# Moving the start of the table lookup on TensorE in a two-layer graph network from slot 19 to slot 12

## What is computed

```
msgs = z[edge_dst] @ Wd + z[edge_src] @ Ws + edge_weight[:, None] * ww[None, :] + bm
agg = segment_max(msgs, edge_dst);  hidden = relu(z @ W1a + agg @ W1b + b1);  out = hidden @ W2 + b2
x = layernorm(x + out)
x = layernorm(x + sage(x))      # two mean aggregations over the same edges, with a relu between
```

## Time and profile before

| | us |
|---|---|
| median of three runs (1100.16 to 1101.87) | 1100.61 |
| the profiled execution | 1098.6 |
| its span, from the first to the last instruction | 1096.8 |
| TensorE busy in the span | 1020.9 |
| VectorE busy | 852.8 |
| POOL busy | 739.7 |
| ScalarE busy | 671.0 |

### The profile page before, as it was taken

One profiled execution on the slowest core, in us unless ns is written; L12 is line 12 of the kernel. 1 busy time (PEld: TensorE's weight loads), 2 busy tenths in 40 slices (PEclk: granted clock), 3 DMA queues, 4 the chain that ended last, 5 costly groups with the idle time before them and its releaser, 6 DMA issues.

```text
span 1096.8 us, 25699 instructions
## 1 busy us (share of the span) xinstructions
PE 1020.9 (93%) x7183; PEld 756.1 (69%) x7183; DVE 852.8 (78%) x2994; ACT 671.0 (61%) x1741; POOL 739.7 (67%) x782
## 2 busy tenths in 40 slices
PE   4898989999999999999999999998988989899997
PEld 4576667777777777776767777766666666657786
DVE  6598788888878878887979888987877877645465
ACT  3345778988887778877867887433233333313664
POOL 7767777777777777777777777777777777201332
PEclk9898999999999999999999999999999999999999
DMA  8654434344334434434444443543444353545321
GB/s 204 166 130 114 96 98 103 94 100 119 95 102 106 107 104 107 101 94 128 107 102 92 104 94 98 144 107 88 115 132 104 101 148 99 147 127 164 80 59 42
DMA packets 130203, 121.29 MB, mean 111 GB/s; under 512 B 24126, under 2 KB 115573, under 8 KB 130053
## 3 DMA queue, kind: packets, MB, share of 16 engines
q1 hardware_dynamic: 103624, 70.53, 24.5%
q0 software_dynamic: 23328, 47.82, 18.0%
q10 hardware_dynamic: 3101, 1.21, 0.5%
HBM read 105.60 MB, written 13.88 MB: 109 GB/s over the span
## 4 chain that ended last, share of the span: by engine, by line
PE 48%; POOL 27%; issue 13%; ACT 4%; DVE 3%; DMA 2%; ACTq 2%; DVEq 0%; SPq 0%
POOL area L1100 27%; PE bank L1833 9%; PE bank L1735 8%; PE bank L1959 7%; PE bank L1724 5%; PE bank L1802 4%; PE bank L1675 4%; PE bank L1714 3%; PE bank L1663 2%; PE bank L1924 2%; ACT area L949 1%; PE bank L1910 1%; DMA area<-zs_d,area 1%; ACT hot_r L957 1%; ACTq L889 1%
## 5 line engine op out<-in xcount | busy, mean ns | idle before, releaser
L1100 POOL DMA_INDIRECT area<-zs_d,area x701 | 679.7, 970 | 216.4 <-issue 210.9
L896 ACT CAST adj_w<-bank 128x325 f32 x391 | 176.6, 452 | 312.7 <-PE bank L1735 244.7
L1286 DVE TENSOR_TENSOR_SCAN area<-area,bank 128x512 f32<-128x512 bf16 x196 | 249.6, 1274 | 141.1 <-PE bank L1675 122.2
L1270 DVE TENSOR_SCALAR area<-area 128x325 bf16<-128x325 f16 x782 | 252.2, 323 | 0.0
L1735 PE MATMUL bank<-area 128*128 128x104 f32 x1564 | 225.1, 287 | 0.2
L1269 DVE TENSOR_SCALAR area<-area 128x128 bf16<-128x128 f16 x782 | 209.3, 268 | 5.4 <-PE bank L1735 5.3
L1735 PEld LDWEIGHTS bank<-area 128*128 128x128 f32 x1564 | 196.1, 197 | 10.6 <-issue 2.0
L1833 PE MATMUL bank<-hot_r,zs_r 128*128 128x512 f32 x600 | 176.1, 420 | 1.9 <-ACT hot_r L957 1.2
L1724 PE MATMUL bank<-area 128*128 128x325 bf16 x782 | 151.5, 307 | 9.8 <-DVE area L1271 5.4
L949 ACT ACTIVATE area<-adj_w,node_c 128x512 bf16<-128x512 f32 x225 | 156.5, 744 | 0.0
L1675 PE MATMUL bank<-ident,area 128*128 128x128 f32 x706 | 117.1, 289 | 27.5 <-DMA area<-zs_d,area 27.1
(11 more groups left out here) (175 smaller groups left out, 1105.9 us busy)
## 6 DMA issues: line engine op xcount, KB each, us to landing
area<-mask_d SPq DMA_DIRECT2D x195, 128.0 KB
area<-zs_d,area POOLq DMA_INDIRECT x701
area<-zs_d SPq DMA_DIRECT2D x640, 0.5 KB
area<-parts_d SPq DMA_DIRECT2D x20, 384.0 KB, 6.8
area<-wp_d SPq DMA_DIRECT2D x195, 9.0 KB
adj_w<-in_src_dram SPq DMA_DIRECT2D x12, 256.0 KB
zr_d<-area SPq DMA_DIRECT2D x24, 128.0 KB
area<-zr_d SPq DMA_DIRECT2D x6, 512.0 KB, 3.9
```

Source lines behind the costliest of these rows:

```text
L896: nc.scalar.copy(adj[:, :, bass.ds(at, W)], A_BANK[s % 2][:, 0:COLS].rearrange("p (h w) -> p h w", w=W))
L1100: pool.indirect_dma_start(gring[:, g % GR * 4 + s % 2 * 2 + u, :], None, x if g < RAW else zs_d[0:N, :], bass.IndirectOffsetOnAxis(ap=firs ...
L1270: nc.vector.tensor_scalar(hot_d[:, r, u, :], i_key[:, 0:COLS], key_n[:, u, s:s + 1], None, ALU.is_equal)
L1286: nc.vector.tensor_tensor_scan(S[:, g % 2, 0:n], mask[:, g % MR, 0:n], (G_BANK if g in PICKED else T_BANK[g % 2])[:, 0:n], S[:, (g + 1) % ...
```

## The change

Thirteen groups are picked instead of twelve, and picking begins in slot 12 instead of slot 19. Every picked group but the first still begins where the one before it ends. The four pieces of `zs` are loaded in slots 5 to 8 and split in slots 7 to 11. The one-hots of the first two picked groups are all made by ScalarE.

```diff
-PICKS = ((28, 19), (37, 28), (46, 37), (55, 46), (66, 55), (77, 66), (88, 77), (99, 88), (110, 99), (121, 110), (132, 121), (143, 132))
+ENDS = (21, 30, 39, 47, 56, 67, 78, 89, 100, 111, 122, 133, 144)
+PICKS = tuple(zip(ENDS, (12,) + ENDS))
 PICKED = tuple(g for g, _ in PICKS)
-SPLITS = ((11, 0, 8), (13, 8, 16), (15, 16, 24), (16, 24, NT))
-SOURCE_SLOTS = (8, 10, 12, 13)
+SPLITS = ((7, 0, 8), (8, 8, 16), (10, 16, 24), (11, 24, NT))
+SOURCE_SLOTS = (5, 6, 7, 8)
...
 def by_vector(u):
-    return u % 4 == 3
+    return u >= 2 * NT and u % 4 == 3
```

## The result

The changed kernel takes **1115.63 us** (median of 6 runs, 1111.79 to 1116.71) against 1100.78 us for the kernel before in the same session: a ratio of **1.0131, 95% interval 1.0116 to 1.0147**, 14.9 us slower. The forecast was 1106.6 us, with 1112.5 as the upper end of its range. The profiled execution after took 1116.55 us, its span is 1114.7 us, 17.9 us longer than the span before; the two traces show 3 us more than the medians, since the execution profiled before lay 2.0 us under its median and the one after 0.9 us over its own.

The account below looks back on a forecast made before the run. POOL, hardly ever waiting, was taken to bound the kernel, TensorE in step in the middle. 9.3 - 2.4 - 0.9 = 6.0 us slower gave 1104.6 profiled, 1106.6 us as median (2.0 above); range 1097.5 to 1112.5.

Parts of the forecast that it names:

- the ring: The ring of four groups between POOL's gathers and TensorE: forgives 0.9 us of TensorE's lateness at slot 119.
- Where it starts: ScalarE's end of slot 11: 85.9 us instead of 84.24, a split gone and two one-hots added.
- the third rival: Slots 7 to 9: edge weights land behind the pieces on SP's queue, up to 5.5 us more, 1112.1; chance 0.10.
- no row shows such a wait: Argument against edge weights landing late behind the pieces: the earlier profile had no such wait, loads standing slots apart.
- Slots 12 to 28: ScalarE's copies, 48 one-hots, small work and two register reads in these 17 slots: 91.7 us.
- the lateness at slot 30: TensorE's entry into slot 30 against the kernel before: 178.5 us against 169.25, 9.3 us late.
- Won back until slot 119: Slots 30 to 119: TensorE's 2.3 + 2.0 us of gather waits go, less 1.9 us of picks: 2.4 us.
- the 0.13 of a group: Added picking between slots 30 and 56, priced on TensorE at 0.13 x 14.3 = 1.9 us.
- the signs that the prediction named: Slots 12 to 28 taking 5 us and longer, TensorE waiting on `hot_r`, POOL's waits growing around slot 32, clock 1.00.
- The first: Rival: POOL's four fewer gathers decide, the end comes 5.1 us sooner, 1095.5; chance 0.17.
- The second rival: No change: 3 to 4 us lateness at slot 30, forgiven by stretch and ring, 1098.5 to 1102.8; chance 0.13.
- The rule against the change: A relu or compare belongs on VectorE: the 12 one-hots would cost 5.7 us there instead of 13.7 on ScalarE.

Follow-up runs that it names:

- the run with nine slots: The changed kernel with its third pick in nine slots instead of eight: 1114.43 us, ratio 1.0137.
- the loads alone: The kernel before with the source table loaded in slots 5 to 8 and split in slots 7 to 11, picking still from slot 19: 1101.17 us, ratio 1.0014.
- two versions with 0.2 and -0.3 us there: The changed kernel with every third one-hot on VectorE throughout, 1098.66 us, ratio 0.9990; the same with the third pick in nine slots, 1098.13 us, ratio 0.9988.
- group 60: The kernel before with one gather instead of four in group 60, in the middle: 1099.41 us, ratio 1.0000.

## Why the prediction was off

Direction and mechanism held up to slot 30: ScalarE's one-hots make TensorE late, POOL waits for it, the ring forgives little. The forecast's 6.0 us were 17.9 in the traces. Three terms were mis-sized, the fourth a little. The largest step that failed is the recovery between slots 30 and 119: 2.4 us were to come back, 4.0 us more were lost.

**Where it starts: 85.9 us, measured 89.0, 3.1 us.** The loads and splits were costed at nothing, since TensorE is far behind POOL there. That cover hides a landing from POOL; ScalarE's work of slots 10 and 11 stands behind TensorE's and has no such cover. The timeline of TensorE after, slots 9 and 10:

```profile
72.12 0.38 PE L1664 MATMUL bank<-area,ww 9*128 9x512 bf16 x1 [1.03 <-DMA area<-wp_d]
...
74.55 0.72 PE L1725 MATMUL bank<-area 128*128 128x325 bf16 x2 [1.16 <-DVE area L1272]
...
75.14 2.01 PE L1736 MATMUL bank<-area 128*128 128x104 f32 x8
...
77.91 0.38 PE L1664 MATMUL bank<-area,ww 9*128 9x512 bf16 x1
...
79.33 1.12 PE L1736 MATMUL bank<-area 128*128 128x104 f32 x8
```

Slot 9's edge weights are 1.03 us late. That is the third rival's place, at a fifth of its bound (5.5 us), but not its mechanism: SP issued them only at 70.33 us, where the kernel before did it at 68.60, and slot 9 begins 1.79 us after the issue, so they did not land behind a piece. The kernel before has such a wait too, in slot 11; the prediction's "no row shows such a wait" was a misreading. SP's row after, and slot 11 of TensorE before:

```profile
70.33 0.28 SPq L526 DMA_DIRECT2D area<-wp_d  x1
...
78.40 0.39 PE L1663 MATMUL bank<-area,ww 9*128 9x512 bf16 x1 [1.95 <-DMA area<-wp_d]
```

Then VectorE's low split stands ahead of the flags of a slot and TensorE waits 1.16 us for it, and behind that idle time it runs at the lower clock level. ScalarE's timeline after shows what reaches it in slots 10 to 12, and the first copy of slot 29 at the far end:

```profile
81.67 0.46 ACT L897 CAST adj_w<-bank 128x325 f32 x1 [3.07 <-issue]
...
83.22 1.08 ACT L939 CAST zs_r<-adj_w 128x1024 fp32r<-128x1024 f32 x1
...
84.69 0.48 ACT L897 CAST adj_w<-bank 128x325 f32 x1
...
87.86 1.15 ACT L958 ACTIVATE hot_r<-area 128x512 fp32r<-128x512 bf16 x2
90.83 0.44 ACT L897 CAST adj_w<-bank 128x325 f32 x1 [1.82 <-PE bank L1736]
...
183.46 0.43 ACT L897 CAST adj_w<-bank 128x325 f32 x1
```

The 3.07 us of "issue" ahead of the copy at 81.67 are a read of sixteen registers, which comes in slot 10 as it does in slots 18 and 26. From its end ScalarE waits for no other engine until it has written the last one-hot of slot 11, from 87.86 to 89.01: the third split (83.22) and the first source numbers have filled its pause, so that slot 11's first copy, at 84.69, starts at once, and TensorE waits for ScalarE's copies in that slot (0.43 and 0.20 us). In the run with nine slots, the same code up to here, the stretch begins 2.2 us earlier:

```profile
79.50 0.46 ACT L897 CAST adj_w<-bank 128x325 f32 x1 [2.77 <-PE bank L1736]
```

There the read lies under a wait for TensorE, and ScalarE ends slot 11 at 86.86 us, 1.0 us behind the forecast. So about 1.0 of the 3.1 us is in both executions, the work of slot 10 that the sum left out, and 2.1 us are in this one alone. With the loads alone the time moved by 1.0014: the lateness costs little by itself. What it costs with ScalarE's full slots behind it no run shows separately; the two executions, 2.1 us apart at the end of slot 11 and 3.6 in slot 30, speak for it.

**Slots 12 to 28: 91.7 us, measured 183.46 - 89.01 = 94.5, 2.8 us.** ScalarE's waits from 89 to 183.3 us after:

```profile
ACT adj_w L897 <- issue: 5.2, 2, 2.6
...
ACT adj_w L897 <- PE bank L1736: 2.8, 3, 1.8
```

The two register reads cost the 5.2 us that the sum had. The 2.8 us are waits for TensorE, which the sum left out; the longest is the 1.82 us in slot 12, behind the late start. From there to slot 30 it is 0.98 us, for 0.94. So the lateness at slot 30 was 9.3 + 3.1 + 2.8 = 15.2 us, as the trace has it. In the run with nine slots, where slots 12 to 28 took ScalarE 179.86 - 86.86 = 93.0 us, it was 9.3 + 1.0 + 1.3 = 11.6.

**Won back until slot 119: 2.4 us, measured 4.0 us lost, 6.4 us.** The waits for gathers did go. TensorE's and its weight loads' waits after, slot 30 to slot 119:

```profile
PE bank L1725 <- ACT area L898: 4.7, 11, 1.1
PE bank L1834 <- ACT hot_r L958: 1.2, 3, 0.6
PE bank L1725 <- DVE area L1272: 1.0, 3, 0.4
...
PEld bank L1834 <- ACT hot_r L958: 5.6, 14, 0.9
```

None of them is a gather any more; in the kernel before the first and the last of these rows were 2.9 and 3.3 us. The 4.3 us that the prediction took from the earlier trace rows were waits of weight loads; TensorE's matmuls waited for gathers less, slot 30 to slot 119 before:

```profile
PE bank L1675 <- DMA area<-zs_d,area: 2.7, 3, 1.2
```

The busy time of that stretch (PE, PEld, DVE, ACT, POOL), before:

```profile
169.00:583.00 414.00, 407.03 (x2889) 301.31 (x2887) 344.25 (x1242) 334.67 (x845) 315.54 (x324) 1.00 0.42 105
```

After, and with every third one-hot on VectorE:

```profile
184.00:602.00 418.00, 410.30 (x2890) 303.10 (x2890) 341.48 (x1242) 338.23 (x852) 308.41 (x318) 1.00 0.42 103
...
169.41:583.60 414.19, 408.96 (x2881) 303.63 (x2890) 351.94 (x1263) 319.70 (x813) 313.74 (x322) 1.00 0.42 104
```

TensorE was busy for 98% of it already, with 7.0 us idle in all, so that little could be won back. But TensorE's added work is not what cost the time: with every third one-hot on VectorE the same picks stand in this stretch, TensorE's busy time is 408.96 - 407.03 = 1.9 us longer, just as priced, and it fits into the idle time (0.2 us lost). The prediction priced the 0.13 of a group at TensorE's 1.9 us and left out that ScalarE has to write its one-hots in fewer slots too. Every third one-hot on VectorE takes ScalarE's busy time off that path, 319.70 us for 338.23, and the loss with it: 0.2 us, where it is 5.5 with every fourth and 4.0 in the changed kernel.

**What the ring forgives: 0.9 us, measured 19.2 - 17.9 = 1.3.** The distance from TensorE's entry to POOL's first gather is 603.72 - 602.47 = 1.25 us, where 1.66 was taken from slot 7. The rule itself held roughly: in nine of the ten other kernels the span moved by the lateness at slot 119 within 2.3 us, and the tenth is the one in which gathers were taken out behind that slot.

Sum: 6.0 + 3.1 + 2.8 + 6.4 - 0.4 = 17.9. Of the signs that the prediction named, slots of over 5 us, TensorE waiting on `hot_r` and POOL waiting for TensorE came; the clock in slots 12 to 18 is 0.91 of full, not 1.00, and POOL's waits begin before slot 30 already (14.1 us between 60 and 169 us, 3.1 before).

**The rivals.** The first, POOL's four gathers worth 5.1 us, falls by its own condition: it was to decide from a lateness under 3.3 us at slot 30, and two versions with 0.2 and -0.3 us there gained nothing that can be measured (their intervals end at 3.0 and 3.2 us faster, short of 5.1). The prediction read POOL's few waits as a sign that POOL decides; POOL and TensorE were in step, so that a gain on one alone is stopped by the other, as group 60 shows. The second rival, lateness forgiven, did not come: nothing was forgiven but the ring's 1.3 us. The third had the right place, a fifth of the size, and the wrong cause.

The rule against the change, from the Trainium skill, page "ScalarE: Activation LUTs", section "Rules for kernel authors", that a relu belongs on VectorE (a compare does not stand there), agrees with the traces: back on VectorE, at 0.478 us for 1.145 us each, the first two picks' share took 11.0 of the 15.2 us away behind slot 12. What the prediction hung on it, that the change would then come out at the first rival's gain, did not follow (1.0060).

**No version with all its gathers beats the kernel before** by more than a measurement can tell. A thirteenth group might pay where POOL decides, behind slot 144; that was not tried, since the one-hots share memory with what ScalarE's copies write into `adj_w` there, and so it is not shown.

## What to carry to other kernels

An engine without waits is not the only bound: when two engines go in step, take a few instructions out of one, at two places, and see where that moves the end; here three gathers were worth 0 us in the middle and 3.6 us in the last third. Read the busy share of a long stretch before counting on a wait that goes: in one that is 98% full, the few us of idle time are all that can be won back. And price each moved step on every engine that has a share in it: the picks were priced on TensorE, and ScalarE's share in fewer slots cost more; one-hots moved from ScalarE to VectorE had a price on POOL.

## What was not expected of the hardware

TensorE's clock made one of the differences between executions of the same code. In slot 9 the changed kernel ran eight matmuls on L1736 in 2.01 us, half the rate of the 1.12 us one slot later. The version with nine slots, alike up to there, waited as long at that place and did not slow down; its timeline:

```profile
73.97 0.45 PE L1725 MATMUL bank<-area 128*128 128x325 bf16 x2 [1.20 <-DVE area L1272]
74.29 1.12 PE L1736 MATMUL bank<-area 128*128 128x104 f32 x8
...
75.78 0.38 PE L1664 MATMUL bank<-area,ww 9*128 9x512 bf16 x1
```

From that wait's end to the next slot it takes 75.78 - 73.97 = 1.81 us, the changed kernel 77.91 - 74.55 = 3.36 us. The granted clock from 74 to 81 us is 1.00 here and 0.76 there, a mean between the two levels of 1.2 and 2.4 GHz. Ahead of it TensorE had waited 0.79 us for slot 9's edge weights here and 1.03 us there, so that nearly the same waits were followed by different levels. The Trainium skill, page "TensorE: Matmul & The Clock Gate", section "What's actually happening", says that activity releases the throttle and that the number of slow matmuls varies from run to run of the same kernel; the two traces agree. Here it is 1.5 us in one slot, near the 2.2 us that can be told from no change at all.
